# Attention and feed-forward layer on one core: attention's remainder in 64x32 row tiles, feed-forward bias added by VectorE, first tile projected unsplit, a new order of stages

## The reference

```python
def _layernorm(x): ...                      # mean and variance over the 256 columns
x = x + _layernorm(attn(_layernorm(x)))
x = x + _layernorm(ffn(_layernorm(x)))

def attn(x):                                # has its own layernorm with ln_w, ln_b
    q, k, v = h @ w_q, h @ w_k, h @ w_v     # 16 heads of 16
    q, k = rope(q), rope(k)
    t = 1 + s + 0.5 * s * s                 # s = q k / 4
    return (t / sum(t)) v, heads side by side, @ w_o

def ffn(x):                                 # blocks of 32 share a scale, values on an FP6 grid
    return quantize(x) @ quantize(weight).T + bias
```

## Time and profile before

| | us |
|---|---|
| median of 3 runs (lowest, highest) | 674.09 (673.84, 676.11) |
| the profiled execution, its span | 673.7, 671.8 |
| TensorE busy in the span | 660.0 (98%) |
| VectorE | 562.8 (84%) |
| ScalarE | 558.0 (83%) |
| GpSimd | 335.2 (50%) |

### The profile page before, as it was taken

One profiled execution on the slowest core, in us unless ns is written; L12 is line 12 of the kernel. 1 busy time (PEld: TensorE's weight loads), 2 busy tenths in 40 slices (PEclk: granted clock), 3 DMA queues, 4 the chain that ended last, 5 costly groups with the idle time before them and its releaser, 6 DMA issues.

```text
span 671.8 us, 20456 instructions
## 1 busy us (share of the span) xinstructions
PE 660.0 (98%) x6772; PEld 505.7 (75%) x6772; DVE 562.8 (84%) x1460; ACT 558.0 (83%) x1551; POOL 335.2 (50%) x723
## 2 busy tenths in 40 slices
PE   7889999999999999999999999999999999999998
PEld 6766677777777777877777787777778777777578
DVE  5998889888988888898888889888888988986675
ACT  4578999798898979888897988889798888989864
POOL 3654435545554554555455455545544554643354
PEclk8999999999999999999999999999999999999999
DMA  7101100202011010201101020111102001010101
GB/s 236 33 3 32 34 1 3 80 17 81 9 49 48 30 60 18 79 11 48 50 32 58 17 81 9 49 48 37 55 17 80 11 18 49 9 50 23 51 33 40
DMA packets 28165, 28.35 MB, mean 42 GB/s; under 512 B 1824, under 2 KB 27936, under 8 KB 28064
## 3 DMA queue, kind: packets, MB, share of 16 engines
q1 hardware_dynamic: 27248, 26.26, 12.2%
q10 hardware_dynamic: 816, 0.79, 0.4%
HBM read 18.65 MB, written 8.39 MB: 40 GB/s over the span
## 4 chain that ended last, share of the span: by engine, by line
PE 94%; DVE 2%; ACT 2%; issue 1%; POOL 1%; DVEq 0%; POOLq 0%; ACTq 0%
PE ps_f L635 11%; PE ps_mt L796 10%; PE ps_o L687 9%; PE ps_o L690 8%; PE ps_qk L591 5%; PE ps_qk L594 5%; PE ps_qk L592 4%; PE ps_w L591 4%; PE ps_w L592 4%; PE ps_w L594 4%; PE ps_tr L658 4%; PE ps_tr L591 4%; PE ps_o L724 4%; PE ps_tr L594 2%; PE ps_tr L592 2%; PE ps_tr L672 2%
## 5 line engine op out<-in xcount | busy, mean ns | idle before, releaser
L944 ACT ACTIVATE feat<-ps_f 128x512 f32<-128x512 f32 x256 | 153.1, 601 | 1.8 <-PE ps_f L635 1.1
L635 PE MATMUL ps_f<-qT,selr 128*128 128x512 f32 x320 | 136.1, 428 | 0.7 <-ACT feat L944 0.5
L527 DVE TENSOR_TENSOR kf<-kf 128x1024 f32<-128x1024 f32 (+1 forms) x128 | 135.7, 1095 | 0.2
L1488 POOL TENSOR_TENSOR ve_y<-var_y,epst 128x1 f32<-128x1 f32 x64 | 24.4, 382 | 167.0 <-ACT squares_y L1048 167.0
L796 PEld LDWEIGHTS ps_mt<-kf,vp 128*32 128x32 f32 x2048 | 65.5, 110 | 38.6 <-issue 35.5
L796 PE MATMUL ps_mt<-kf,vp 128*32 128x161 f32 x2048 | 82.2, 301 | 0.1
L991 ACT ACTIVATE hT<-ps_tr,small,lnwx 128x128 f32<-128x128 f32 x128 | 51.6, 454 | 24.5 <-PE ps_tr L672 23.7
L687 PE MATMUL ps_o<-feat,main 128*32 128x512 f32 x512 | 68.2, 603 | 0.0
L690 PE MATMUL ps_o<-feat,rm 128*32 128x512 f32 x512 | 67.0, 592 | 0.0
L635 PEld LDWEIGHTS ps_f<-qT,selr 128*128 128x128 f32 x320 | 60.3, 189 | 8.7 <-issue 4.7
L1488 POOL TENSOR_TENSOR ve_f<-var_f,epst 128x1 f32<-128x1 f32 x64 | 14.5, 227 | 103.6 <-ACT squares_f L1067 103.6
(11 more groups left out here) (194 smaller groups left out, 1989.9 us busy)
## 6 DMA issues: line engine op xcount, KB each, us to landing
xc<-L_attn_x SPq DMA_DIRECT2D x16, 512.0 KB, 4.0
result<-fin SPq DMA_DIRECT2D x64, 128.0 KB, 1.7
xa<-L_attn_x SPq DMA_DIRECT2D x15, 512.0 KB, 4.0
wkqv<-L_attn_w_kv ACTq DMA_DIRECT2D x2, 256.0 KB, 4.8
xa<-L_attn_x SPq DMA_DIRECT2D x1, 384.0 KB, 6.3
csel<-selection SPq DMA_DIRECT2D x1, 320.0 KB, 6.7
wkqv<-L_attn_w_q ACTq DMA_DIRECT2D x1, 256.0 KB, 4.4
wf<-L_ffn_weight SPq DMA_DIRECT2D x1, 256.0 KB, 6.1
```

The lines of the kernel that those rows point to most:

```text
L527: return eng.tensor_tensor(dims(row, F_MAIN, [[FW, heads], [HD, NR], [1, HD]]), dims(row, F_LIN, [[FW, heads], [0, NR], [1, HD]]), dims(ro ...
L635: pe.matmul(ps_f[i % 2][:, :], selr[:, i], qT[:, par, quad], start=True, stop=True).then_inc(sel_done, 1)
L944: act.activation(feat[:, p2, i], ps_f[i % 2][:, :], ACT.Square).then_inc(squared, 1)
```

## The change

- **attend**: the 512 columns of a quad are two parts of 256. The main half is one matmul per part and head; part 0 goes to `ps_o`, part 1 to `ps_w`. The rest uses 64 of the array's 128 rows: in part 0 heads 0 and 1 use rows 0 to 63 and heads 2 and 3 rows 64 to 127, in part 1 the other way round. `rm_moved` holds the weights with their halves exchanged (two DMAs after `copy_rest`, on ScalarE's queue), and `select_4` is two matmuls of 256 columns, the second with a selection that puts the heads into the exchanged rows. `copy_quad` copies two halves. `attend` now waits for `ps_w`, and `project_out` for `copy_quad`.
- **ffn**: no bias matmul; always in `ps_qk`; VectorE's new `add_bias` adds the bias row into `fb` in SBUF, from which `square_f` and `add_ffn` read. `ffn` waits for `rope_cos` and `rope_sin`, `project_kq` for `add_bias`. The constants for the bias matmul and their setup go.
- **first tile**: `project_kq` and `project_v` of tile 1 use fp32 inputs and weights whole (`whole_product`); `high_h` and `low_h` skip it.
- **order**: all tables `LAG`, `FIRST` and `FINAL` and the lists in each `step` are new. TensorE's list is shown below; its lags are turn_attention 12, project_out 13, select_4 7, turn_q 3, project_kq 1, turn_z 0, rest_matrix 3, select_0 to select_3 6, turn_quads 11, turn_ffn_input 15, ffn 16, sum_features 2, attend 7, project_v 0, turn_sums 2. VectorE's is stats_x, moments_x, rope_add, low_ffn_input, rest_terms, block_maxima, extend_k, products_1, constant, normalise_x, products_0, from_grid, scales, low_attention, inverse_scales, rope_cos, rope_sin, add_ffn, invert_denominators, add_attention, normalise_attention, add_bias, to_grid. ScalarE's is square_f, high_q, copy_quad, square_2, copy_v, square_3, copy_main, high_attention, square_4, copy_q, square_y, square_k, copy_h, copy_rest, high_h, square_s, square_0, high_ffn_input, square_1, centre, copy_sums.

```diff
+        quad_bank = [ps_o, ps_w]
...
+        rm_moved = sb("rm_moved", [P, 2, NQ, P])
...
-        def ffn_bank(t):
-
-            return ps_qk if t.n > TILES - NT * 2 else ps_w
...
-                pe.matmul(ps_f[i % 2][:, :], selr[:, i], qT[:, par, quad], start=True, stop=True).then_inc(sel_done, 1)
+                if i < HQ:
+                    pe.matmul(ps_f[i % 2][:, :], selr[:, i], qT[:, par, quad], start=True, stop=True).then_inc(sel_done, 1)
+                else:
+
+                    for part in range(2):
+                        mm = pe.matmul(ps_f[0][:, part * TH:(part + 1) * TH], selr[:, HQ + part], qT[:, par, quad, part * TH:(part + 1) * TH],
+                                       start=True, stop=True)
+                    mm.then_inc(sel_done, 1)
...
+                wait(pe, xs_ready, issued["project_out"])
+                wait(pe, wdt_copied, CH * issued["turn_ffn_weight"])
                 pe.wait_ge(rm_copied, t.seq + 1)
+                pe.wait_ge(rest_moved, 32 * (t.seq + 1))
                 pe.wait_ge(squared, CHUNKS * (n + 1))
-                for h in range(HQ):
-                    pe.matmul(ps_o[VW * h:VW * (h + 1), :], main[:, par, quad, VW * h:VW * (h + 1)], feat[:, p2, h],
-                              start=True, stop=False, skip_group_check=True)
-                for h in range(HQ):
-                    mm = pe.matmul(ps_o[VW * h:VW * (h + 1), :], rm[:, par, quad, VW * h:VW * (h + 1)], feat[:, p2, HQ],
-                                   start=False, stop=True, skip_group_check=True)
+                for part in range(2):
+                    for h in range(HQ):
+                        pe.matmul(quad_bank[part][VW * h:VW * (h + 1), 0:TH], main[:, par, quad, VW * h:VW * (h + 1)],
+                                  feat[:, p2, h, part * TH:(part + 1) * TH], start=True, stop=False, skip_group_check=True)
+                for part in range(2):
+                    for h in range(HQ):
+
+                        half = (h // 2 + part) % 2
+                        rows = slice(64 * half, 64 * half + 64)
+                        weights = (rm, rm_moved)[part]
+                        mm = pe.matmul(quad_bank[part][VW * h:VW * (h + 1), 0:TH], weights[rows, par, quad, VW * h:VW * (h + 1)],
+                                       feat[rows, p2, HQ, part * TH:(part + 1) * TH], start=False, stop=True, skip_group_check=True)
...
+            def whole_product(out_, x, w):
+
+                for c in range(CH):
+                    mm = pe.matmul(out_, x(c), w(c), start=c == 0, stop=c == CH - 1)
+                return mm
...
             def project_kq(t):
                 p2 = t.two
                 if t.n == 1:
+                    pe.wait_ge(wkq_in, 2 * 16)
+                    pe.wait_ge(hT_copied, 1)
+                    whole_product(ps_qk[:, :], lambda c: hT[:, c], lambda c: wkqv[:, c, 0:2 * D]).then_inc(qk_done, 1)
+                    return
+                if t.n == 2:
                     pe.wait_ge(wkq_high, 1)
                     pe.wait_ge(wkq_low, 1)
-                pe.wait_ge(hT_low, t.n)
+                pe.wait_ge(hT_low, t.n - 1)
 
                 wait(pe, qk_read, 2 * (t.n - 1))
+                wait(pe, f_biased, issued["ffn"])
...
             def ffn(t):
                 p2 = t.two
                 if t.n == 1:
-                    pe.wait_ge(bias_done, 1)
-                    pe.wait_ge(ones_cast, 1)
                     pe.wait_ge(wdt_high, CH)
                     pe.wait_ge(wdt_low, 1)
                 pe.wait_ge(xdT_low, t.n)
-                if t.n > TILES - NT * 2:
-
-                    pe.wait_ge(qk_read, 2 * TILES)
-                    wait(pe, fin_ready, t.n - 1)
-                else:
-                    wait(pe, xs_ready, issued["project_out"])
-                    wait(pe, fin_ready, issued["ffn"])
-                pe.matmul(ffn_bank(t)[:, 0:D], ones[:, :], bias2[:, :], start=True, stop=False)
-                split_product(ffn_bank(t)[:, 0:D], lambda c: xdT_h[:, p2, c], lambda c: xdT_l[:, p2, c],
-                              lambda c: wdt_h[:, c], lambda c: wdt_l[:, c], bias=True).then_inc(ffn_done, 1)
+                wait(pe, qk_read, 2 * issued["project_kq"])
+                wait(pe, f_biased, issued["ffn"])
+                split_product(ps_qk[:, 0:D], lambda c: xdT_h[:, p2, c], lambda c: xdT_l[:, p2, c],
+                              lambda c: wdt_h[:, c], lambda c: wdt_l[:, c]).then_inc(ffn_done, 1)
 
             def project_out(t):
                 p2 = t.two
...
                     pe.wait_ge(wo_low, 1)
                 pe.wait_ge(aT_low, t.n)
                 wait(pe, xs_ready, issued["project_out"])
-                wait(pe, fin_ready, min(issued["ffn"], TILES - NT * 2))
+                wait(pe, o_copied, issued["attend"])
...
             def step(n):
+                each(n, "turn_attention", turn_attention)
+                each(n, "project_out", project_out)
+                each(n, "select_4", select, 4)
                 each(n, "turn_q", turn_q)
                 each(n, "project_kq", project_kq)
                 each(n, "turn_z", turn_z)
+                once(n, "rest_matrix", rest_matrix)
                 each(n, "select_0", select, 0)
+                each(n, "turn_quads", turn_quads)
                 each(n, "select_1", select, 1)
+                each(n, "turn_ffn_input", turn_ffn_input)
+                each(n, "ffn", ffn)
+                each(n, "sum_features", sum_features)
+                each(n, "attend", attend)
+                each(n, "select_2", select, 2)
+                each(n, "project_v", project_v)
+                each(n, "select_3", select, 3)
+                once(n, "turn_sums", turn_sums)
...
+                act.wait_ge(rm_copied, t.seq + 1)
+                for half in range(2):
+                    act.dma_start(rm_moved[64 * half:64 * half + 64, mpar], rm[64 - 64 * half:128 - 64 * half, mpar]).then_inc(rest_moved, 16)
...
-                act.activation(osb[:, par, quad], ps_o[:, :], ACT.Identity, bias=cb[:, par, quad:quad + 1]).then_inc(o_copied, 1)
+                for part in range(2):
+                    ins = act.activation(osb[:, par, quad, part * TH:(part + 1) * TH], quad_bank[part][:, 0:TH], ACT.Identity,
+                                         bias=cb[:, par, quad:quad + 1])
+                ins.then_inc(o_copied, 1)
...
-                act.wait_ge(ffn_done, t.n)
+                act.wait_ge(f_biased, t.n)
                 wait(act, rstd["f"], t.n - 2)
-                act.activation(squares["f"][:, t.two], ffn_bank(t)[:, 0:D], ACT.Square, scale=ROOT,
+                act.activation(squares["f"][:, t.two], fb[:, t.two], ACT.Square, scale=ROOT,
                                accum_out=var["f"][:, t.two:t.two + 1]).then_inc(f_squared, 1)
...
+            def add_bias(t):
+                if t.n == 1:
+                    dve.wait_ge(bias_centred, 1)
+                dve.wait_ge(ffn_done, t.n)
+
+                wait(dve, fin_ready, t.n - 2)
+                dve.tensor_tensor(fb[:, t.two], ps_qk[:, 0:D], b2c[:], ALU.add).then_inc(f_biased, 1)
+
             def add_ffn(t):
                 dve.wait_ge(rstd["f"], t.n)
 
                 wait(dve, stored[t.two], 16 * ((t.n - 1) // 2))
-                dve.scalar_tensor_tensor(fin[:, t.two], ffn_bank(t)[:, 0:D], rs["f"][:, t.two:t.two + 1], xs[:, t.four],
+                dve.scalar_tensor_tensor(fin[:, t.two], fb[:, t.two], rs["f"][:, t.two:t.two + 1], xs[:, t.four],
                                          ALU.mult, ALU.add).then_inc(fin_ready, 1)
```

More of the change, by code:

```diff
@@ L64 @@
 LAG = {
-    "fill_a": 0, "warm_up": -19, "turn_ffn_input": 15, "rest_matrix": 4, "fill_b": 2, "drain_a": 16, "attend": 8,
-    "sum_features": 3, "project_v": 1, "select_2": 7, "turn_attention": 12, "turn_sums": 3, "ffn": 15, "select_3": 7,
-    "turn_q": 3, "select_4": 7, "project_kq": 1, "turn_ffn_weight": 12, "turn_quads": 11, "turn_z": 0, "drain_b": 14,
-    "select_0": 6, "project_out": 12, "select_1": 6,
-    "high_kq": -20, "high_v": -20, "centre": 14, "square_f": 16, "square_3": 8, "copy_q": 4, "split_wo": -4,
@@ new lines @@
+    "project_kq": 1, "turn_z": 0, "drain_b": 18, "rest_matrix": 3, "turn_ffn_weight": 6, "select_0": 6, "fill_a": 0,
+    "fill_b": 1, "turn_quads": 11, "select_1": 6, "turn_ffn_input": 15, "ffn": 16, "sum_features": 2, "attend": 7,
+    "select_2": 6, "project_v": 0, "select_3": 6, "turn_sums": 2,
+    "high_kq": -20, "high_v": -20, "square_f": 17, "high_q": 2, "cast_selection": -16, "sum_bias": -18,
+    "centre_bias": -16, "copy_quad": 8, "square_2": 7, "copy_v": 1, "weight_size": -14, "square_3": 7,
@@ new lines @@
+    "turn_z": (-19, -16, -16, -15, -13, -13, -12, -11, -9, -7, -3, -1),
+    "rest_matrix": (0, 0, 0, -12, 0, 0, 0, -4, 0, 0, 0, 0),
+    "select_0": (-12, -12, -10, -8, -4, -2, -1, 0, 0, 0, 0, 0),
+    "fill_a": (-14, -17, -17, -22, -19, -16, -21, -18, 0, 0, 0, 0),
+    "fill_b": (-18, -12, -23, -11, -22, -23, -22, -25, 0, 0, 0, 0),
```

(23 more changed lines are left out.)

442 lines of the change are left out of this document (201 added, 241 removed).

## The result

The changed kernel takes 680.85 us (median of 4 runs, 680.11 to 681.71), the kernel before beside it 674.23 (673.84 to 676.11): a ratio of 1.0093, 95% interval 1.007 to 1.0116. It is slower by 0.9%, where 667 us had been forecast. The profiled execution took 681.07 us, its span is 679.3 us.

A forecast was written before the change was run, and what follows sets the result against it. TensorE, busy 500 of 500 us between 100 and 600, was taken as the bound. Sixteen sequences at -0.36 us gave -5.8, with the start -6.8: from 674.1 to 667 us, range 654 to 686, likeliest 660 to 671.

The forecast's parts named there:

- The step that failed: rm_moved's two transfers on ScalarE's queue behind copy_rest: cost nothing; if late, attend and all of TensorE behind it would wait.
- its cover is gone only if ACT is over a microsecond behind: Shared bank ps_w, from attend through copy_quad to the next project_out: 1.5 us for a copy_quad of about 1, costed at nothing.
- Rest against a new change of shape: TensorE's attend, per tile: rest on eight 64x32 tiles saves 0.43 us, change of shape between main and rest costs 0.15.
- Bias matmul: TensorE's ffn, per tile: dropping it saves 0.12 us of its 0.20; the next product pays the 0.08 for following transposes.
- Wait ahead of turn_ffn_input and ffn: TensorE stands 0.27 us until rope_cos and rope_sin have read ps_qk, in three tiles of four; bounds 0 and 0.5.
- Per sequence: Four tiles at -0.38 us, +0.35 for rest_matrix's own changes of shape, three waits of 0.27: -0.36 us; sixteen sequences -5.8.
- The end: Last 28 us: ffn's bank freed earlier against about 3 us more VectorE work from add_bias; taken as 0, bounds -4 and +4.
- (a): Rival: in attend's rest, matmuls of different row halves writing one bank take turns, +0.43 us per tile: 695 us; chance 0.12.
- (b): Rival: no wait at ffn, 654 us; with the change of shape at 0.03 as well, 647; chance 0.17.
- (c): Rival: about the same time; ffn's wait at 0.4 us or the new change of shape at 0.23: 672 to 674; chance 0.20.
- (d): Rival: slower through VectorE or ScalarE, waits for copy_quad, low_ffn_input or add_attention, 0.3 us per tile: 686, or 680; chance 0.10.
- The forecast of 8.8 us per tile: VectorE's busy time: 8.40 us a tile plus 0.41 for add_bias, 8.8 of a period of 9.4, close but no bound.

The follow-up runs named there:

- the version with SyncE's issues: The changed kernel with rm_moved's two transfers issued by SyncE, which waits for rm_copied, and no longer by ScalarE: 667.44 us, ratio 0.9889.

## Why the prediction was wrong

**The step that failed.** "Its two small transfers for rm_moved are issued in ACT's queue behind copy_rest; attend first needs them a whole step later, so I cost them at nothing". I asked who waits for the data and not who stands behind the issue. The data are in time: they land 2.4 us after the issue (median). ScalarE's queue is what they cost: 1.27 us of ScalarE once per sequence. It became TensorE's loss at the place that I had dismissed with "its cover is gone only if ACT is over a microsecond behind": ScalarE is 1.27 behind, of which some 0.6 is still covered, copy_quad is late, and the next to write the bank, turn_attention, stands (I had named project_out, which comes just behind it). The price is 680.85 - 667.44 = 13.4 us. Of the 14.4 us between the spans (679.3 and 664.9), 8.0 arise in the 40 tiles from the 16th attend to the 56th: it starts at 192.33 and 588.03 in the changed kernel, at 187.87 and 575.56 in the version with SyncE's issues. 3.0 more arise between the first attend and the 16th and 1.9 between the 56th and the last. Tile by tile, 15 tiles, one in every four, lose 12.3 us of this: 0.65 to 0.91 each, except one with 1.29 and one with 1.67. The last 1.5 us lie ahead of the first attend (54.00 against 52.52), where ScalarE stands once too; but versions with the same start and without that stall have their first attend anywhere from 52.5 to 53.6, so they can't be given to it.

**The rest of the sum held in total, not in every part.** Without that term it gave 667, and the kernel without that stall measures 667.44. Term by term, with the traces of the kernel before and of the version with SyncE's issues:

- Rest against a new change of shape, forecast -0.43 + 0.15 = -0.28: measured -0.27, the change of shape 0.11. In whole kernels, 682.84 - 667.44 = 15.4 us, 0.24 per tile.
- Bias matmul, forecast -0.12: 0.09 to 0.11, and 0.11 in the old order too (periods of 9.49 and 9.38).
- Wait ahead of turn_ffn_input and ffn, forecast 0.27: from the start of turn_quads to the second product of ffn 408.46 - 407.13 = 1.33, for which the forecast's prices give 0.43 + 0.23 + 0.22 + 0.12 = 1.00, so 0.33, about 0.2 of it ahead of turn_ffn_input. The chain that I had used as a check, copy_h, stands first in the trace.
- Per sequence, forecast -0.36: from the 16th attend to the 56th, ten sequences, it is 387.69 us with SyncE's issues and 579.69 - 188.93 = 390.76 before, so -0.31. Two sizes that make it up are wrong in opposite directions: the period with rest_matrix went from 10.56 to 10.41, where -0.03 had been forecast, and the other three together from 28.52 to 28.36, where -0.33 had been.
- The start, forecast -1: the first attend starts at 52.52 against 52.18 before. No gain shows.
- The end, forecast 0: from the last attend to the last instruction 32.1 us against 30.3 before, so +1.8, inside its bounds; but the eight tiles from the 56th attend to the last take 4.7 us less than before, where the forecast gives 0.7.
- The span, forecast -6.8: 671.8 - 664.9 = 6.9, so close in part by luck: the start gave 1.3 us less than forecast and the 55 tiles behind it 0.5 less, the last eight tiles with the end 2.1 more.

**The rivals.** (a) did not come: heads 0, 1 and heads 2, 3 write one bank from different row halves within 0.02 us. The Trainium skill, TensorEngine Tiling (Array Packing), section Restrictions and Gotchas, says that different row tiles cannot access one PSUM bank simultaneously; the trace disagrees, for tiles in different column groups at least, which is all that runs here. (b) and (c) fall with the measured wait of 0.33 and the change of shape of 0.11. (d) had the right place, waits for copy_quad, and a wrong cause: no lack of slack in general and not in each tile, but one stall of ScalarE in each fourth. Its 680 us is right by luck, since it was made of 4 us at the end, which measured 1.8, and 0.15 in each tile, which doesn't show. I had given it 0.10.

**VectorE.** The forecast of 8.8 us per tile was wrong: it is 487.33 us over some 52 tiles, 9.4, of a period of 9.7 on average. I had added instructions at their old durations, and the new order lengthened the old ones. It changed little, 1.2 to 1.7 us, because VectorE was still a little below TensorE. The Trainium skill states the mechanism, in SBUF — State Buffer, section SBUF: two separate sides: VectorE and GpSimd share one pair of ports, which whichever starts first holds for its whole instruction; on VectorE's side the page names instructions with two inputs in SBUF, against one of GpSimd that reads SBUF, and those in a mode that uses both ports. The trace agrees where it can be seen: from_grid 896 ns beside low_q, and 474 when low_q lies beside reads of PSUM. z, which has one tensor in SBUF, goes from 406 to 683 and starts while products_2, held up behind products_1, is still at work; whether it runs in such a mode no run here shows.

## What to carry to other kernels

A transfer has two prices: when its data land, and what stands behind its issue on the queue that issues it. Price both, and give an issue that needs a result of its own engine either to a queue that has nothing else to do or to a place some instructions further on, where that result is old. VectorE's 96% of busy time was no proof that it was the bound: shorten the busy engine's work and see whether the time follows, before building on it. And when a stage is moved on one engine, its partners on the others have to move along, or each of them stands in its old place.

## What the hardware showed that I had not expected

- Two transfer issues of 64 partitions each held ScalarE's queue for 1.12 us (0.47 to 0.61 each where they stand apart; now and then one took 1.2 to 1.8), and cost ScalarE 1.27 us behind a wait for its own last result, but 0.8 us in the whole kernel where the queue was ahead of the execution. The Trainium skill, Advanced Engine Details and Errata, section Engine Queue Depths, gives ScalarE a queue of 8 on trn2; in the trace the issue is five instructions ahead, which is within it; where the limit lies no run here shows.
- The wait for a result of the instruction just ahead costs ScalarE nothing by itself: high_h starts 0.03 us after copy_rest's end with the wait and 0.02 after it without.
- Eight 64x32 tiles run together, two banks and both row halves: 16 instructions of 256 columns start within 0.29 us, a round 0.24 after the other.
- A change from 128x32 to 64x32 tiles costs 0.11 us, about the same as the way into 128x32 from 128x128 (0.12, estimated from the earlier trace rows).
- VectorE and GpSimd can double each other's durations (475 to 896 ns, 705 to 1347 ns) by order alone, with no instruction changed.
